# Tiles 8 to 63 of the normalised input turned by DMA transposes instead of by TensorE and VectorE

## The reference

```python
xn = (x - mean(x)) / sqrt(var(x) + 1e-5)                 # over the last axis
Q = einsum('bnd,hdk->bhnk', xn, proj_q)                   # 8 heads
K = einsum('bmd,dk->bmk', xn, proj_k)
V = einsum('bmd,dv->bmv', xn, proj_v)
weights = softmax(einsum('bhnk,bmk->bhnm', Q, K))
O = einsum('bhnm,bmv->bhnv', weights, V)
Y = einsum('bhnv,hdv->bnd', O, proj_o)
ffn = einsum('aemn,enh->amh', einsum('amh,ehn->aemn', xn, w1), w2)
out = x + Y + ffn
```

## Time and profile before

| what | value |
|---|---|
| median of three timed runs | 1643.09 us (1643.03 to 1643.25) |
| the profiled execution's own time | 1643.02 us |
| its span, first to last instruction | 1641.2 us |
| TensorE busy | 1625.0 us (99%) |
| TensorE weight loads (beside the products) | 1206.0 us (73%) |
| VectorE busy | 1238.2 us (75%) |
| ScalarE busy | 1301.1 us (79%) |
| GpSimd busy | 1380.2 us (84%) |
| DMA: bytes moved, mean rate | 16.73 MB, 10 GB/s |
| granted TensorE clock | 0.999 of full |

### The profile page before, as it was taken

The page is one execution under the profiler, slowest core; times in us unless marked ns, Lnnn a source line. Parts: engine busy times, 40 slices in busy tenths (PEclk is TensorE's granted clock), DMA queues, the critical chain, the costliest instruction groups (busy, mean ns, idle before and its releaser), DMA issues.

```text
span 1641.2 us, 46471 instructions
## 1 busy us (share of the span) xinstructions
PE 1625.0 (99%) x18798; PEld 1206.0 (73%) x18798; DVE 1238.2 (75%) x2661; ACT 1301.1 (79%) x1348; POOL 1380.2 (84%) x1008
## 2 busy tenths in 40 slices
PE   8999999999999999999999999999999999999998
PEld 6777777777777777777777777777777777777775
DVE  6777777777777777777777777777777777777775
ACT  4788887888888888888888878888888887878885
POOL 3688888888888888888888888888888888888786
PEclk9999999999999999999999999999999999999999
DMA  8000000000000000000000000000000000000000
GB/s 234 2 2 2 2 2 14 2 2 2 2 15 2 2 2 8 8 2 2 2 8 8 2 2 2 8 8 2 2 2 8 8 2 2 2 15 2 1 2 14
DMA packets 16769, 16.73 MB, mean 10 GB/s; under 512 B 432, under 2 KB 12976, under 8 KB 16560
## 3 DMA queue, kind: packets, MB, share of 16 engines
q1 hardware_dynamic: 15520, 13.24, 2.8%
q10 hardware_dynamic: 1040, 0.52, 0.1%
HBM read 9.57 MB, written 4.19 MB: 8 GB/s over the span
## 4 chain that ended last, share of the span: by engine, by line
PE 97%; DVE 1%; ACT 1%; issue 0%; ACTq 0%; POOL 0%; DVEq 0%
PE s_ps L575 14%; PE s_ps L590 14%; PE s_ps L588 14%; PE t_ps L630 13%; PE t_ps L633 13%; PE t_ps L632 13%; PE s_ps L463 4%; PE s_ps L465 4%; PE s_ps L464 4%; PE t_ps L612 2%; PE t_ps L603 1%; PE t_ps L645 0%; PE s_ps L603 0%; PE s_ps L700 0%; PE s_ps L699 0%; ACT pr_hi L426 0%
## 5 line engine op out<-in xcount | busy, mean ns | idle before, releaser
L328 POOL TENSOR_TENSOR pr_lo<-pr,pr_hi 128x1024 f16<-128x1024 f32 x511 | 1080.0, 2135 | 233.5 <-ACT pr_hi L426 233.5
L419 ACT ACTIVATE pr<-s_ps,boost,scale 128x1024 f32<-128x1024 f32 x512 | 617.0, 1205 | 199.6 <-PE s_ps L590 199.5
L845 DVE TENSOR_REDUCE key_max<-s_ps 128x128 f16<-128x1024 f32 x512 | 624.1, 1219 | 0.2 <-PE s_ps L575 0.2
L426 ACT ACTIVATE pr_hi<-pr 128x1024 f16<-128x1024 f32 x512 | 525.4, 1051 | 8.1
L588 PE MATMUL s_ps<-g_lo,xT 128*128 128x128 f16 x4096 | 512.4, 219 | 0.9 <-DVE g_lo L858 0.9
L590 PE MATMUL s_ps<-g_hi,xT 128*128 128x128 f16 x4096 | 512.3, 219 | 0.0
L588 PEld LDWEIGHTS s_ps<-g_lo,xT 128*128 128x128 f16 x4096 | 400.7, 98 | 31.2 <-DVE g_lo L858 1.4
L590 PEld LDWEIGHTS s_ps<-g_hi,xT 128*128 128x128 f16 x4096 | 400.8, 98 | 29.8
L630 PE MATMUL t_ps<-pr_hi,xn_hi 128*128 128x512 f16 x1024 | 388.1, 379 | 1.8 <-DVE pr_lo L863 1.8
L632 PE MATMUL t_ps<-pr_lo,xn_hi 128*128 128x512 f16 x1024 | 388.1, 379 | 0.0
L633 PE MATMUL t_ps<-pr_hi,xn_lo 128*128 128x512 f16 x1024 | 388.1, 379 | 0.0
(11 more groups left out here) (131 smaller groups left out, 1596.8 us busy)
## 6 DMA issues: line engine op xcount, KB each, us to landing
out_dram<-xacc SPq DMA_DIRECT2D x16, 256.0 KB, 2.3
w_sb<-in_L_ffn_w_dram SPq DMA_DIRECT2D x1, 2048.0 KB, 10.2
pr<-in_L_attn_proj_q_dram ACTq DMA_DIRECT2D x1, 512.0 KB, 4.7
xacc<-in_L_attn_x_dram SPq DMA_DIRECT2D x2, 256.0 KB, 5.1
pr<-in_L_attn_proj_o_dram SPq DMA_DIRECT2D x1, 512.0 KB, 6.6
xacc<-in_L_attn_x_dram SPq DMA_DIRECT2D x1, 384.0 KB, 11.0
xacc<-in_L_attn_x_dram SPq DMA_DIRECT2D x1, 128.0 KB, 6.4
wkv<-in_L_attn_proj_k_dram SPq DMA_DIRECT2D x1, 64.0 KB, 2.9
```

The source lines that it names most:

```text
L328: pool.tensor_tensor(pr_lo[:, u % RING, :], pr32[:, u % PR, :], pr_hi[:, u % RING, :], ALU.subtract)\
L419: act.activation(pr32[:, u % PR, :], both_banks(u), ACT.Exp, bias=boost[:, 0:1], scale=scale[:, 0:1])\
L426: act.activation(pr_hi[:, u % RING, :], pr32[:, u % PR, :], ACT.Copy).then_inc(p_hi_ready, 1)
L845: dve.tensor_reduce(key_max[:, u % 2, :], both_banks(u).rearrange("p (t q) -> p q t", q=P), AX_X, ALU.max).then_inc(keys_max, 1)
```

## The change

TensorE's two transposes per tile, VectorE's copy, and the waits between them are gone for tiles 8 to 63. SyncE issues two DMA transposes per tile in their place, one from `xn_hi` and one from `xn_lo`, each 128x128 of float16 from SBUF to SBUF, into the same columns of `xT`. They raise a new semaphore `xT_in` by 16 each. Before a tile's two DMAs SyncE waits until the tile is normalised, until the DMAs of the tile before have landed, and, from tile 24 on, until the last readers of the columns written over (scores and expert product) are done. TensorE's batch waits look at `xT_in` in place of `xT_ready`. The stores of the results stand in the same queue of SyncE, each batch's pair of stores behind the transposes of one later tile. Tiles 0 to 7 are turned as before.

```diff
+        xT_in = sem("xT_in")
...
-        def turn_tile(n):
-
-            pair, at = divmod(n, 8)
-            if n == 4:
-                return NT
-            return pair + NT if at == 0 and pair >= 1 and pair + NT < TILES else None
+        def turned_in(tiles):
+
+            return 32 * (tiles - NT)
...
-            for b in range(B):
-                for half in range(2):
-                    k = 2 * (b * H + H - 1) + half
-                    first = query_tile(k)
-                    sp.wait_ge(ffn_added, first + HT)
-                    sp.wait_ge(y_added, 2 * k + 2)
-                    sp.dma_start(out_tiles[:, first:first + HT, :], xacc[:, first:first + HT, :]).then_inc(stored, 16)
+            def turn(tile):
+
+                batch = tile // NT
+                at = tile % KEEP
+                sp.wait_ge(xn_ready, tile + 1)
+                if tile > NT:
+                    sp.wait_ge(xT_in, turned_in(tile))
+                if tile >= KEEP:
+
+                    sp.wait_ge(scores_ready, (batch - 2) * 8 * H)
+                    sp.wait_ge(ffn_ps, tile - KEEP + 1)
+                sp.dma_start(xT[:, 0, at * P:(at + 1) * P], xn_hi[:, at, :], transpose=True).then_inc(xT_in, 16)
+                sp.dma_start(xT[:, 1, at * P:(at + 1) * P], xn_lo[:, at, :], transpose=True).then_inc(xT_in, 16)
...
+            for tile in range(NT, AHEAD):
+                turn(tile)
+            for pair in range(PAIRS):
+                if (tile := ln_tile(pair - 1)) is not None:
+                    turn(tile)
+
+                if pair >= H + 1 and (pair - H - 1) % H == 0:
+                    for half in range(2):
+                        store((pair - H - 1) // H, half)
+            for half in range(2):
+                store(B - 1, half)
...
             def project(k):
                 tile = query_tile(k)
-                pe.wait_ge(xT_ready, tile + HT)
+                if tile < NT:
+                    pe.wait_ge(xT_ready, tile + HT)
+                else:
+                    pe.wait_ge(xT_in, turned_in(tile + HT))
...
-                        pe.wait_ge(xT_ready, batch_tile(k) + NT)
+                        if k < 2 * H:
+                            pe.wait_ge(xT_ready, NT)
+                        else:
+                            pe.wait_ge(xT_in, turned_in(batch_tile(k) + NT))
...
-                    if (tile := turn_tile(u - 1)) is not None:
-                        pe.wait_ge(xT_ready, tile + 1)
...
-                if (tile := turn_tile(n)) is not None:
-                    pe.wait_ge(xn_ready, tile + 1)
-                    pe.transpose(turned_part(n)[:, 0:P], xn_hi[:, tile % KEEP, :], ident16[:, :])
-                    pe.transpose(turned_part(n)[:, P:2 * P], xn_lo[:, tile % KEEP, :], ident16[:, :]).then_inc(xT_ps, 1)
...
-            def copy_turned(n, tile):
-                at = (tile % KEEP) * P
-                dve.wait_ge(xT_ps, tile - NT + 3)
-                dve.tensor_copy(xT[:, :, at:at + P], turned_part(n)[:, 0:2 * P].rearrange("p (k c) -> p k c", k=2))\
-                   .then_inc(xT_ready, 1)
...
-                if (tile := turn_tile(n)) is not None:
-                    copy_turned(n, tile)
```

More of the change, by code:

```diff
@@ L254, in attention_ffn @@
         F_CENTRED = 7
-        def turned_part(n):
-            return bank(n + 1, 0)[:, 0:P].bitcast(F16)
         @block.sync
@@ L270, in _, with store @@
             sp.dma_start(xacc[:, 2 * NT:TILES, :], x_tiles[:, 2 * NT:TILES, :]).then_inc(x_in[4], 16)
-            for b in range(B):
-                for half in range(2):
-                    k = 2 * (b * H + H - 1) + half
-                    first = query_tile(k)
-                    sp.wait_ge(ffn_added, first + HT)
-                    sp.wait_ge(y_added, 2 * k + 2)
-                    sp.dma_start(out_tiles[:, first:first + HT, :], xacc[:, first:first + HT, :]).then_inc(stored, 16)
+            def turn(tile):
[9 more added lines that the diff above has]
+                sp.dma_start(xT[:, 1, at * P:(at + 1) * P], xn_lo[:, at, :], transpose=True).then_inc(xT_in, 16)
+            def store(b, half):
+                k = 2 * (b * H + H - 1) + half
+                first = query_tile(k)
+                sp.wait_ge(ffn_added, first + HT)
+                sp.wait_ge(y_added, 2 * k + 2)
+                sp.dma_start(out_tiles[:, first:first + HT, :], xacc[:, first:first + HT, :]).then_inc(stored, 16)
+            for tile in range(NT, AHEAD):
[8 more added lines that the diff above has]
+                store(B - 1, half)
             sp.wait_ge(stored, 16 * 2 * B)
```

## The result

| | before | after |
|---|---|---|
| median of 6 timed runs | 1643.06 us (1642.43 to 1643.25) | 1636.80 us (1636.36 to 1637.31) |
| profiled execution: time, span | 1643.02, 1641.2 us | 1637.05, 1635.2 us |

The ratio is 0.9962, with a 95% interval from 0.9953 to 0.9972: faster by 0.38%, or 6.3 us by the medians and 6.0 us by the spans. The forecast was 1636.7 us.

What follows compares the result with a forecast made beforehand. The prediction took gapless TensorE as the bound: 112 transposes at 0.0563 us save 6.3 us, VectorE's copies, waits, hidden DMAs and contention count zero, so 1643.02 becomes 1636.7 us, range 1635.7 to 1639.3, chance 0.82.

Steps and rivals of the forecast that it cites:

- The bound: From 60 to 1620 us TensorE is busy without a gap, so the time there is the sum of its instructions.
- The price of a transpose: On TensorE, each of 112 removed transposes costs its start-to-start distance, 0.0563 us, not its 219 ns duration; 6.3 us saved.
- The start-up: Two tiles turned in the first 60 us (at 37 and 53 us) count too: 6.3 us saved, 6.1 if neither does.
- VectorE's copies at nothing: Removing 56 VectorE copies of 0.28 us, 15.7 us in all, gains zero; VectorE still idles 0.44 us after one.
- The DMAs hidden: SyncE's two DMA transposes take 3 to 6 us per tile, hidden with over 20 us to spare.
- Contention: Forecast zero; rival: TensorE slowed by share f beside DMAs in flight, losing 258 x f us, deciding from 2.4%; chance 0.06.
- Late tiles: Rival: DMAs over 27.2 us stall TensorE at seven batch starts; above 24.9 per tile SyncE's queue sets pace; chance 0.04.

## Why the prediction was right

- **The bound.** Right, and shown twice over: TensorE's transposes alone carry the gain (put back, 1642.96), and the rest changes nothing.
- **The price of a transpose.** Right: 0.0563 us by distances was forecast, 0.055 us came out by putting them back. The 275 ns of the Trainium skill (TensorE: Matmul & The Clock Gate, Part 4) would have given 31 us as an estimate; as a share of the engine's time the runs decide against it.
- **The start-up.** A small miss. I let both tiles of the start-up count, 0.2 us. The trace after shows none of it: VectorE's maximum comes 0.09 us earlier, at 53.96 in place of 54.05, but the `c_lo` behind it ends when it did before. VectorE's and GpSimd's timelines before, then after:

```profile
54.64 2.91 DVE L958 SCALAR_TENSOR_TENSOR c_lo<-c,inv_scale,c_hi 128x1024 f16<-128x1024 f32 x1
```

```profile
50.16 6.31 POOL L328 TENSOR_TENSOR pr_lo<-pr,pr_hi 128x1024 f16<-128x1024 f32 x3 [7.62 <-ACT pr_hi L426]
```

```profile
53.96 0.29 DVE L870 TENSOR_REDUCE minus_max<-t_ps 128x1 f16<-128x128 f16 x1 [0.37 <-PE t_ps L627]
...
54.55 3.02 DVE L970 SCALAR_TENSOR_TENSOR c_lo<-c,inv_scale,c_hi 128x1024 f16<-128x1024 f32 x1
```

```profile
50.18 6.31 POOL L348 TENSOR_TENSOR pr_lo<-pr,pr_hi 128x1024 f16<-128x1024 f32 x3 [7.63 <-ACT pr_hi L446]
```

  That `c_lo` reads two buffers in SBUF, began 1.9 us before GpSimd's three subtractions ended at 56.49, and took 0.11 us longer than the 2.91 us of before, about what it began earlier. It waits for GpSimd, as the copy out of SBUF did: before and after it ends 1.08 us behind those subtractions (at 57.55 against 56.47, and at 57.57 against 56.49). In the traces of all ten other kernels it does the same within 0.01 us, while its own duration goes from 2.56 to 3.04 us. The spans differ by 6.0 us, which is 54 tiles at 0.112 us, the prediction's lower bound of 6.1 without the two.
- **VectorE's copies at nothing.** Right, by the run with copies out of PSUM. The 0.44 us of idle time behind a copy that carried the estimate were the right row for a copy of 0.28 us; the copy of 1.82 us overran them and reached TensorE.
- **The DMAs hidden.** Right. I took 3 to 6 us per tile; it is 3.5 us. The 1309 ns that the Trainium skill gives for a transpose by DMA (VectorE: DVE Perf Modes, The three transpose paths), as an estimate 2.6 us for two, is in the right range, and 2.2 to 2.4 us is what one took to land here.
- **Contention.** The forecast's zero holds: the time is the same with none, with 112 and with 672 transposes. Its rival needed 2.4% by the prediction's 258 us in flight, or 2.9% by the 220 us of the trace, and the run with 672 leaves it 0.07% by the medians, 0.3% by the interval.
- **Late tiles.** Its upper bound of 97 us per tile was far off: it took a packet for each of the 16384 elements of a transpose, and there are 160. But its mechanism is real and comes where the prediction put it, past 24.9 us per tile: at 18 us the time stands, at 33.7 us it is 2136.

## What to carry to other kernels

Where one engine runs without a gap, price what you take from it by the distance between its instructions' starts, and price what you give to another engine or queue by the slack of the first instruction that waits for it there, not by that engine's idle share. A DMA transpose moved off a full TensorE is free while its 2.4 us have cover and its issue stands in a queue with nothing urgent behind it. The same 112 DMAs cost 85 to 92 us on ScalarE's queue, and eight behind a large load and without cover cost 23 us. When you put a part back as a control, keep its source memory the same.

## What I had not expected of the hardware

- A VectorE copy from SBUF to SBUF that started during a GpSimd subtraction ended 0.15 us behind it, in all of 56 cases, and so took a median of 1.86 us. A copy from PSUM took 0.28 us in each of 56 cases.
- Issuing a DMA transpose takes its queue 1.09 us alone and 1.23 us behind another, and up to 2.7 us now and then (124 of 1344 took over 1.5 us). Behind the issue of a 3 MB load in the same queue it took 11.4 us.
- After waits of tens of us TensorE restarted at half of its clock. In the run with twelve times the transposes, the window from 1918 to 1921 us has a granted clock of 0.50, the 1.2 GHz level, and 1921 to 1924 has 1.00 again:

```profile
1918.00:1921.00 3.00, 3.00 (x22) 2.16 (x21) 2.07 (x5) 0.00 (x0) 0.00 (x0) 0.50 0.02 5
1921.00:1924.00 3.00, 3.00 (x31) 1.98 (x30) 1.90 (x4) 2.23 (x2) 0.00 (x0) 1.00 0.01 3
```
